# A graph layer on one core: more edges counted instead of gathered, count columns shared between two engines, and a new slot plan

## The reference

```python
def _L0_gnn_ref(node_feats, src, dst, eps, W1, b1, W2, b2, gamma, beta):
    neigh = jax.ops.segment_sum(node_feats[src], dst, num_segments=n)
    h = (1.0 + eps) * node_feats + neigh
    h = jax.nn.relu(h @ W1 + b1) @ W2 + b2
    ...                      # batch norm over the nodes
x = x + gnn(_layernorm(x), src, dst, ...)
x = x + ffn(_layernorm(x))   # 8 experts, top 1, capacity, 256 -> 1024 -> 256
```

## Time and profile before

| | |
|---|---|
| median of the runs | 2540.54 us |
| profiled execution, its own time | 2542.99 us |
| its span | 2541.3 us |
| PE busy | 1732.8 us (68%) |
| DVE busy | 1437.6 us (57%) |
| ACT busy | 694.7 us (27%) |
| POOL busy | 1705.9 us (67%) |
| gathers of POOL (L794) | 1240, 1187.1 us busy, 957 ns mean |
| DMA, mean | 142 GB/s |

### The profile page before, as it was taken

How to read it: one execution, slowest core, us unless ns; L and a number is a source line. 1 busy time by engine, 2 the same in 40 slices (tenths; PEclk the granted TensorE clock), 3 DMA queues, 4 the chain that set the end, 5 groups by cost and what they waited for, 6 DMA issues and landing times. The chain is left out here.

```text
span 2541.3 us, 32604 instructions
## 1 busy us (share of the span) xinstructions
PE 1732.8 (68%) x9046; PEld 1094.2 (43%) x9047; DVE 1437.6 (57%) x4225; ACT 694.7 (27%) x1116; POOL 1705.9 (67%) x1690
## 2 busy tenths in 40 slices
PE   0054455665666666667768677777886789889984
PEld 0022223333333333334334334446884556656663
DVE  7897632556237525632652333335664786867885
ACT  6910000100010001101201111115674545455543
POOL 1177777777777777777777777732564767667864
PEclk9988678877887787778879888896667989999998
DMA  7644456545754565466446533326753212221130
GB/s 228 244 135 120 122 189 221 158 123 156 238 186 122 176 233 159 123 196 204 127 152 208 159 105 105 106 52 217 232 164 112 89 36 71 96 83 57 62 101 13
DMA packets 186690, 361.08 MB, mean 142 GB/s; under 512 B 47285, under 2 KB 111115, under 8 KB 186502
## 3 DMA queue, kind: packets, MB, share of 16 engines
q0 software_dynamic: 69152, 185.00, 24.4%
q1 hardware_dynamic: 115206, 172.60, 20.6%
q10 hardware_dynamic: 2144, 1.05, 0.2%
HBM read 291.08 MB, written 71.92 MB: 143 GB/s over the span
## 5 line engine op out<-in xcount | busy, mean ns | idle before, releaser
L794 POOL DMA_INDIRECT halves<-table,halves x1240 | 1187.1, 957 | 407.0 <-issue 365.2
L885 PE MATMUL e_sums<-halves 128*128 128x256 f16 x1920 | 367.3, 372 | 542.1 <-DMA halves<-table,halves 352.4
L885 PEld LDWEIGHTS e_sums<-halves 128*128 128x128 f16 x1920 | 242.7, 131 | 673.5 <-DMA halves<-table,halves 386.3
L1102 DVE SCALAR_TENSOR_TENSOR nodes<-e_sums,above,nodes 128x256 f32 (+1 forms) x161 | 77.4, 481 | 580.8 <-PE e_sums L885 391.6
L1769 POOL TENSOR_TENSOR x_midl<-x_midf,x_midh 128x512 f16<-128x512 f32 x200 | 294.2, 1497 | 109.0 <-ACT x_midh L1903 103.9
L1859 PE MATMUL x_down<-halves,x_midh 128*128 128x256 f16 x1472 | 248.3, 277 | 14.4 <-DVE x_yb L1996 12.8
L1008 ACT ACTIVATE e_hT<-e_up 128x1024 f32<-128x1024 f32 (+1 forms) x25 | 25.2, 1006 | 850.8 <-PE e_up L934 850.8
L1835 PE MATMUL x_up<-x_xTh,halves 128*128 128x512 f16 (+1 forms) x800 | 232.8, 370 | 3.2 <-ACT x_midh L1903 3.2
L1166 DVE TENSOR_TENSOR counts<-counts,e_tally 128x490 f32 x220 | 159.6, 726 | 121.5 <-PE e_tally L913 115.2
L1859 PE MATMUL x_down<-halves,x_midl 128*128 128x256 f16 x736 | 203.4, 276 | 0.0
L1116 DVE TENSOR_SCALAR halves<-ring,e_rel 128x128 f16 x960 | 175.0, 274 | 31.5 <-DVE e_rel L1110 31.3
(11 more groups left out here) (208 smaller groups left out, 2625.0 us busy)
## 6 DMA issues: line engine op xcount, KB each, us to landing
w1f<-table SPq DMA_DIRECT2D x120, 512.0 KB, 4.5
halves<-table,halves POOLq DMA_INDIRECT x1240
slot_rows<-halves SPq DMA_DIRECT2D x64, 268.0 KB, 3.3
x_row<-slot_rows SPq DMA_DIRECT2D x32, 536.0 KB, 7.0
table<-halves SPq DMA_DIRECT2D x25, 512.0 KB, 3.0
counts<-in_x SPq DMA_DIRECT2D x24, 512.0 KB, 4.8
r_xin<-in_x SPq DMA_DIRECT2D x24, 512.0 KB, 5.1
out<-r_row SPq DMA_DIRECT2D x24, 512.0 KB, 3.4
```

Source lines behind the costliest of these rows:

```text
L794: pool.indirect_dma_start(got[:, r, t, :], None, table.rearrange("p h d -> (p h) d"), bass.IndirectOffsetOnAxis(ap=idx[:, h, r * GT + t:r ...
L885: ins = nc.tensor.matmul(sums[:, place, 0:D], hot[:, place, t, :], got[:, r, t, half * D:(half + 1) * D], start=(t == 0 and half == 0), st ...
```

## The change

- 404 tiles are counted instead of 328, in seven units (152, 64, 50, 41, 36, 32 and 29 tiles), and 1159 gathered, in 145 groups, the last of seven tiles (`TAIL`); padded tiles are no longer gathered.
- From tile 343 (`WIDE`) on a counted tile has 7 target columns; its 686 sums lie in two banks of PSUM, PE writes them with two matmuls of 343, and there are two such places in place of four.
- Of a group's columns only the first is added by DVE, since only it can be shared with the group before. The other 4 (or 6) belong to this group alone, and ACT writes them (`take`, a copy from PSUM to `counts`). DVE waits for the group's take before its add, and PE waits for take and add before it uses the place again.
- ACT clears `counts` in 14 parts of 7 source blocks, each as soon as the pieces that read them are done.
- The tables are replaced by a planner (`Slots`), which fills slot by slot by costs of its own: up to 4 pieces a slot, 6 to 8 tiles (5 wide ones), one piece in a slot with a product of a quad. Half of a slot's pieces stand ahead of the group's matmuls.
- A quad's rows are transposed straight from `nodes`; the copy on DVE (L1210) is gone. In a slot PE runs the product with W2 first, then the transposes, then the product with W1.
- The smallest target of a group (`least`) is subtracted from all of `cold` once, in the plan.

```diff
-UNIT_TILES = ((24, 24, 24, 24, 16, 16, 16), (14, 14, 12, 12, 12), (12,) * 4, (10,) * 4, (11, 11, 10))
-GROUPS = ((96, 4), (168, 2), (328, 1))
+UNITS = (152, 64, 50, 41, 36, 32, 29)
+WIDE = FIRST[5]
+GROUPS = ((96, 4, 5), (168, 2, 5), (WIDE, 1, 5), (HT, 1, 7))
-SINGLE = 40 * RG
+SINGLE = 36 * RG
-MIX = 4
-PIECES = 2
-AT = {2: (9, 2), 3: (13, 1), 4: (16, 1), 5: (19, 1), 6: (21, 2), 7: (24, 0), 8: (26, 1), 9: (28, 2), 10: (30, 2),
...
+PIECES = -(-HI // XK)
+CLOSE = {2: 19, 3: 30, 4: 39, 5: 48, 6: 55, 7: 63, 8: 69, 9: 76, 10: 82, 11: 88, 12: 94, 13: 99, 14: 104, 15: 109,
+         16: 114, 17: 118, 18: 123, 19: 127, 20: 132, 21: 136, 22: 140, 23: 144}
+TENSOR_ROOM, VECTOR_ROOM = 980, 960
...
+            tensor = 300 + 130 * (slot in self.turn) + 710 * (slot in self.up) + 700 * (slot in self.down)
+                    vector += 110 if tile >= WIDE else 65 + 31 // GROUP_OF.count(GROUP_OF[tile])
...
+                n = min(max(1, min(4, (TENSOR_ROOM - tensor) // 120)), PIECES - piece)
...
-                    nc.tensor.matmul(tally[:, group % BANKS, 0:KEY], tall[:, t % OR, KEY:OH], tall[:, t % OR, 0:KEY],
+                    if start and group >= BANKS:
+                        pe.wait_ge(s_taken, group - (2 if group >= WIDE_GROUP else BANKS) + 1)
+                        pe.wait_ge(s_count, group - (2 if group >= WIDE_GROUP else BANKS) + 1)
...
+                def take(group):
+                    width = WIDTH_OF[GROUP_OF.index(group)]
+                    column = act.value_load(plan.cols[0:1, group:group + 1], min_val=0, max_val=P - 1)
+                    act.wait_ge(s_tile, OR + last_tile(group) + 1)
+                    if group > 0:
+                        act.wait_ge(s_taken, group)
...
+                    nc.scalar.activation(counts_at(group, act.snap(column + 1), width - 1), tallied(group)[..., 1:width],
+                                         ACT.Identity).then_inc(s_taken, 1)
...
                     dve.wait_ge(s_tile, OR + last_tile(group) + 1)
+                    dve.wait_ge(s_taken, group + 1)
-                    nc.vector.tensor_tensor(place, place, tally[:, group % BANKS, 0:KEY].rearrange("p (k d) -> p k d", d=TW),
-                                            ALU.add).then_inc(s_count, 1)
+                    nc.vector.tensor_tensor(place, place, tallied(group)[..., 0:1], ALU.add).then_inc(s_count, 1)
...
-                    nc.vector.tensor_scalar(hrow.rearrange("p t d -> p (t d)"), nodes[:, q, :], 1.0, None,
-                                            ALU.mult).then_inc(s_hrow, 1)
...
+                    early = 0 if slot in SLOTS_OF.fold else len(pieces) // 2
+                    for number in pieces[:early]:
+                        piece(number)
                     if slot < SINGLE:
                         gathered_once(slot)
...
+                    for number in pieces[early:]:
+                        piece(number)
```

More of the change, by code:

```diff
@@ L56 @@
 HG = _group
-SINGLE = 40 * RG
+WIDE_GROUP = GROUP_OF[WIDE]
+SINGLE = 36 * RG
 NG = -(-(ET - HT) // GT)
@@ L101 @@
[L101 to L110, removed]
+assert EP % PT == 0 and HT % PT == 0 and HI * P >= N and NARROW <= 2 * D and 0 < TAIL <= GT
@@ L113, in closed_before @@
+SLOTS_OF = Slots()
+ORDER = [q for _, q in sorted(SLOTS_OF.turn.items())] + [NQ - 1]
+LATE = range(NG, SLOTS_OF.end)
+assert sorted(ORDER) == list(range(NQ)) and max(SLOTS_OF.spread) < NG
 def closed_before(group):
-    return max([0] + [QN * (q + 1) for q, (it, r) in AT.items() if it * RG + r <= group])
-assert _at <= NIT and _tile == HT and max(SPREAD) <= min(AT[0], AT[1])[0]
-HOT_END = QN * 2
+    return max([0] + [QN * (q + 1) for slot, q in SLOTS_OF.turn.items() if slot <= group])
 BOUNDS = []
@@ L279 @@
     unit: object
-    least: object
     above: object
@@ L538, in sources @@
                 dve.sem_inc(s_rows, 1)
-                then(nc.vector.scalar_tensor_tensor(out=kone, in0=high, scalar=float(TW), in1=ends[:, hot_to],
-                                                    op0=ALU.mult, op1=ALU.add))
+                for a, b, width in ((0, WIDE, 5), (WIDE, HT, 7)):
+                    also(nc.vector.scalar_tensor_tensor(out=kone[:, a:b], in0=high[:, a:b], scalar=float(width),
+                                                        in1=ends[:, hot_to][:, a:b], op0=ALU.mult, op1=ALU.add))
+                dve.wait_ge(s_rng, link[0])
             def windows():
@@ L790, in _, with gather @@
                 nc.gpsimd.memset(zero[:, :], 0.0).then_inc(s_zero, 1)
-                def gather(h, r):
-                    for t in range(GT):
+                def gather(h, r, tiles=GT):
+                    for t in range(tiles):
                         pool.indirect_dma_start(
@@ L903, in gathered @@
                                                        got[:, r, t, half * D:(half + 1) * D],
-                                                       start=(t == 0 and half == 0), stop=(t == GT - 1 and half == 1))
+                                                       start=(t == 0 and half == 0), stop=(t == tiles - 1 and half == 1))
                         ins.then_inc(s_sum, 1)
@@ L979, in _ @@
-                for step in LATE:
-                    quad_steps(step)
+                    pieces = SLOTS_OF.pieces.get(slot, ())
+                    early = 0 if slot in SLOTS_OF.fold else len(pieces) // 2
+                    for number in pieces[:early]:
+                        piece(number)
+                    if slot < SINGLE:
+                        gathered_once(slot)
+                    else:
+                        gathered(slot // RG, slot % RG)
+                    if slot in SLOTS_OF.spread:
+                        for t in tiles:
+                            count(t)
@@ L1034, in _ @@
                 act.dma_start(W2s[:, :, :], W2.rearrange("(k p) f -> p k f", p=P)).then_inc(s_w, 16)
+                act.wait_ge(s_zero, 1)
                 blank(0)
-                for n in range(NIT):
-                    if n in SPREAD and SPREAD[n] + 1 < NU:
-                        blank(SPREAD[n] + 1)
-                    for r in range(RG):
-                        quad_steps(n * RG + r)
-                for step in LATE:
-                    quad_steps(step)
+                for slot in range(NG):
+                    before = max([0] + [pieces[-1] + 1 for at_slot, pieces in SLOTS_OF.pieces.items() if at_slot < slot])
+                    blank(before)
+                    for t in SLOTS_OF.tiles.get(slot, ()):
+                        if t == last_tile(GROUP_OF[t]):
+                            take(GROUP_OF[t])
+                    quad_steps(slot)
+                for slot in LATE:
+                    quad_steps(slot)
                 columns(NQ - 1, LAST)
```

378 lines of the change are left out of this document (213 added, 165 removed).

## The result

The changed kernel takes 2568.09 us (median of 4 runs, 2564.54 to 2568.70); the kernel before took 2541.59 beside it (4 runs). The ratio is 1.0096, with a 95% interval of 1.0078 to 1.0115: it is 1% **slower**, where 2491 us was forecast, 2450 to 2538 with the bounds. The profiled execution took 2568.59 us with a span of 2566.8.

The account below looks back on a forecast made before the run. POOL's issuing of gathers was taken as the bound: 2542.99 − 102.2 (fewer gathers) + 1.5 (one-hots) + 45 (waiting for PE) + 6 (end) = 2493.3, less 2.45 to the median: 2491 us, range 2450 to 2538.

Parts of the forecast that it names:

- the room of 15 us: Edge stage: PE may run some 15 us late before POOL must wait; lag beyond that is lost for good.
- the ledger: Slot-by-slot sum of PE's lag against 10.09 us a slot: +45 us of POOL waiting for PE.
- 81 gathers: POOL in the edge stage: 1159 gathers instead of 1240, −102.2 us; slower gathers beside more one-hots, +1.5 us.
- Rival 4: DVE blocks POOL in the edge stage: +31 us instead of +1.5, so 2510 us; chance 0.03.
- Four pieces, one piece and product: PE's late slots with pieces: 11.3 us with four pieces, 10.1 with one piece and a quad's product.
- rival 2: Slots of four pieces: landing from 5.2 us makes them 12.9 us, the loss 100 us, the kernel 2546; chance 0.10.
- Tile slot, 7.3 us: Late PE slot of six counted tiles, DVE setting its length: 7.3 us; five wide tiles the same.
- Tile slot with a product, 14.1 us: Late PE tile slot with a quad's product: 13.6 us before, +0.5 for ACT's takes, 14.1 (13.6 to 15.6).
- Rival 3: Tile slots: ACT's takes chain; at 1.0 us each a product slot costs 15.6, loss 67, 2513 us; chance 0.15.
- The end: After the last gathers: a second window in the last group and later transposes, +6 us, between 3 and 8.

## Why the prediction was wrong

- **The method held.** POOL's gathers were the bound, POOL waited for PE alone, and the room of 15 us works. But the first pause of over 0.6 us comes ahead of group 30 (3.1 us), after the first burst of pieces, where the forecast had none before slot 60; and by group 90 some 58 us had been lost, where the ledger had 9.
- **81 gathers:** forecast −102.2 + 1.5, measured −106.2 in the sum above, of which some 4 are the rounding of the gap; the pitch without pauses did not change. Rival 4 (DVE blocks POOL) fell: the mean gather took 958 ns, against 957. The rule of the Trainium skill quoted in the prediction ("SBUF — State Buffer", section "SBUF: two separate sides") does not show here: with the one-hots of 76 more tiles a gather was no longer. Whether these one-hots run in the mode that the rule is about, no run shows.
- **Four pieces, one piece and product:** right in the sum (649 us against 654), not in its parts, so partly by luck. I had assumed a landing of 4.4 and 0.3 from use to issue; the landing alone was 4.7. A piece took PE 216.0 × 4 / 686 = 1.26 us on average, not 0.95. From one slot of four pieces to the next it was 13.0 us (mean of 22, first slots of a burst left out) and not 11.3, about what rival 2 had priced. What came out cheaper were the edges, since half of a slot's pieces stand ahead of its group: a product with three pieces took 11.3, and six slots with transposes and two pieces left took 6.3. Rival 2 fell as an account of the loss: the landing stayed under its 5.2, and the bursts as a whole took no longer than forecast.
- **Tile slot, 7.3 us: this step failed.** "With an add of 98 sums, which no row shows: nothing to 0.57, I take 0.2, as it has a fifth of the elements". The add doesn't scale with its elements: 591 ns for 98 against 726 for 490. The pitch of a tile on DVE was 0.92 and not 0.61, so a late slot of six tiles took 9 to 10 us. "Five wide tiles come to the same" failed too: with five wide tiles it was 12.2 without transposes and 12.2 and 13.3 with them, where I had 7.3 and 8.4; without the take the same three took 10.9, 9.4 and 11.3. The add's share of the pitch is 0.92 − 0.41 = 0.51 us, near the far end of my own range.
- **Tile slot with a product, 14.1 us: this step failed as well.** I gave the takes "+0.5". They made it 16.3 with narrow tiles and 18.5 with wide ones; without them it is 14.4 and 16.0, so the take cost 2 to 2.5 us, about the far end (15.6 in total) and beyond. I had counted how long a take lasts, not where it stands: behind ACT's work for the quad and ahead of DVE's add, with only two places for wide sums. Rival 3 named this mechanism and priced it at a loss of 67; it would have given 2513.
- **The ledger with the measured prices** (9.5 for a tile slot, 6.8 more with a product, all else as it was) gives 131 us of lost time; measured is 128, 123 without the rounding of the gaps. It puts 38 of the 131 into the bursts of pieces, where 34 were measured. So close an agreement is partly luck: with the wide slots at their measured 12.2 and 18.5 the ledger gives 160. With 9.5 and my 14.1 it gives 93, with 7.3 and 16.3 it gives 77. Each mistake alone would have left the kernel near 2525 to 2540. They add up more than singly because the room was used up already: once PE is a full 15 us late, each microsecond of a slot over 10.09 is lost in full.
- **The end:** +6 forecast, +3.3 measured behind the last gather.
- **The chances.** I put rivals 2 and 3 side by side as if only one could be true, and only for one kind of slot each. No case held both errors of the tile slots at once, though both rested on instructions that no row showed.

## What to carry to other kernels

Don't price a small operation that no row shows by its elements; take the nearest row in full until there is one of its own. Here a fifth of the elements cost four fifths of the time. Handing part of a step to an idle engine puts a hand-over into the chain, behind whatever that engine does in its own order. (More places between the engines might have helped; that was not tried.) Where one engine's pace is the bound and the others run near it, where the work stands decides: with the same 404 tiles the kernel took 2568 or 2471 us, by two costs in the planner.

## What the runs showed of the hardware

A DVE add of 1, 98, 490 and 686 values a partition (PSUM in, strided f16 out) took 161, 591, 726 and 889 ns. The last three are 98 separate places a partition with 1, 5 and 7 neighbouring values each. So a place with one value cost (591 − 161) / 97 = 4.4 ns, and each further value in it 0.3 to 0.8. By these four rows the change left out the cheap values and kept the 98 dear places; that is an estimate, as no run has 98 values side by side. The Trainium skill ("VectorE: DVE Perf Modes", section "The TRN2 errata") says that VectorE and ScalarE instructions that read SBUF pay a fixed extra cost each, so that small operands lose most by it. From 490 values to 98 the rows agree in kind: 392 elements fewer, 135 ns less. A fixed cost doesn't explain the 591, though: the same instruction with one value took 161.

On four of six chips every kernel that also ran elsewhere, the one before too, was 13 to 16% longer, with engines idle where the profile names no engine of this core as the releaser. The mean granted TensorE clock of the profiled executions was 0.80 to 0.81 there and 0.83 to 0.85 on the others, but GpSimd's mean gather was as long as ever (958 ns in the changed kernel on both kinds). Waits of DVE in the changed kernel on such a chip, from 120 to 1980 us:

```profile
DVE nodes L1195 <- remote: 226.1, 29, 24.6
DVE w2f L1245 <- remote: 64.8, 12, 11.0
```

In the changed kernel's first profile no wait has such a releaser. What holds the engines there was not found.
